# A fused token-mixing and ternary-FFN kernel: a one-power scale for four tiles' statistics, a later wait for the ternary weights, and a prologue with its work dealt out anew

## What is computed

```python
x = L0_attn_x                                   # 8 batches x 1024 tokens x 512 channels, fp32
xn = _layernorm(x)                              # eps 1e-5
x = x + attn(xn) + ffn(xn)

def attn(x):                                    # 16 heads
    xs = jnp.pad(x, ((0, 0), (1, 0), (0, 0)))[:, :T]          # the token before
    xm = x * time_mix + xs * (1.0 - time_mix)
    k = jnp.exp(jnp.minimum(xm @ Wk.T, 60.0)); v = xm @ Wv.T; r = xm @ Wr.T
    # Wm: exponential decay over the lag, one rate a head, own weight at lag 0
    wkv = einsum(Wm, k * v); sum_k = einsum(Wm, k) + 1e-16
    return (sigmoid(r) * wkv / sum_k) @ Wo.T

def ffn(x):
    xn = (x - mean) * rsqrt(var + 1e-3) * ln_gamma + ln_beta
    beta = mean(|weight|); w_q = clip(round(weight / (beta + 1e-5)), -1, 1)   # ternary
    gamma = max(|xn|)                           # over the whole tensor
    return clip(xn * 128 / gamma, -128 + 1e-5, 128 - 1e-5) @ w_q * (gamma * beta / 128)
```

## Time and profile before

| | |
|---|---|
| median of 3 runs | 927.05 us (925.34 to 927.47) |
| the profiled execution's own time | 927.5 us |
| its span in the trace | 925.4 us |
| mean granted TensorE clock | 0.994 |
| PE busy | 879.9 us, 95% of the span |
| DVE busy | 762.3 us, 82% |
| ACT busy | 509.6 us, 55% |
| POOL busy | 207.9 us, 22% |

### The profile page before, as it was taken

How to read it: one execution, slowest core, us unless ns; L and a number is a source line. 1 busy time by engine, 2 the same in 40 slices (tenths; PEclk the granted TensorE clock), 3 DMA queues, 4 the chain that set the end, 5 groups by cost and what they waited for, 6 DMA issues and landing times.

```text
span 925.4 us, 12794 instructions
## 1 busy us (share of the span) xinstructions
PE 879.9 (95%) x3984; PEld 714.7 (77%) x3984; DVE 762.3 (82%) x1278; ACT 509.6 (55%) x832; POOL 207.9 (22%) x268
## 2 busy tenths in 40 slices
PE   2889999999999999999899999999999999999998
PEld 2668777777878777777688888888888888888886
DVE  6898888879798898979689787896878968789684
ACT  5473856747574757747355454554445544456451
POOL 6643425144343425232010020110201102011000
PEclk9999999999999999999899999999999999999999
DMA  7222405142321405144335333353233532244211
GB/s 272 92 91 71 157 14 189 37 148 69 136 91 68 159 0 184 55 147 113 116 124 194 137 94 115 121 193 136 91 104 134 193 136 91 94 145 137 91 46 45
DMA packets 59841, 107.13 MB, mean 116 GB/s; under 512 B 7712, under 2 KB 7712, under 8 KB 59808
## 3 DMA queue, kind: packets, MB, share of 16 engines
q1 hardware_dynamic: 59808, 106.73, 33.9%
HBM read 64.76 MB, written 41.96 MB: 115 GB/s over the span
## 4 chain that ended last, share of the span: by engine, by line
PE 56%; DVE 20%; issue 11%; ACT 7%; POOL 4%; DMA 1%; SPq 0%; DVEq 0%; POOLq 0%; ACTq 0%
PE kvr L483 11%; PE kvr L485 11%; PE kvr L484 11%; PE out_banks L520 6%; PE out_banks L518 6%; DVE scans L921 4%; PE out_banks L498 4%; DVE bn_stats L791 3%; PE out_banks L501 3%; PE out_banks L500 3%; DVE rwkv_lo L941 2%; DVE evacuated L840 2%; DVE k_and_kv L911 1%; DVE k_and_kv L937 1%; DVE absmax L847 1%
## 5 line engine op out<-in xcount | busy, mean ns | idle before, releaser
L1162 POOL TENSOR_TENSOR evacuated<-normed,mix_over_ffn_row 128x512 f32<-128x512 f32 x28 | 36.4, 1298 | 360.5 <-DVE ffn_lo L864 360.5
L483 PE MATMUL kvr<-xm_hi,wk_hi 128*128 128x512 f32 x256 | 104.9, 410 | 8.8 <-ACT w_ternary L753 4.4
L483 PE MATMUL kvr<-xm_hi,wv_hi 128*128 128x512 f32 x256 | 103.4, 404 | 0.1
L483 PE MATMUL kvr<-xm_hi,wr_hi 128*128 128x512 f32 x256 | 102.7, 401 | 0.0
L498 PE MATMUL out_banks<-wo_hi,rwkv_hi 128*128 128x512 f32 x256 | 101.9, 398 | 0.5 <-DVE rwkv_lo L941 0.5
L485 PE MATMUL kvr<-xm_hi,wk_lo 128*128 128x512 f32 x256 | 101.8, 398 | 0.0
L484 PE MATMUL kvr<-xm_lo,wk_hi 128*128 128x512 f32 x256 | 101.4, 396 | 0.0
L501 PE MATMUL out_banks<-wo_hi,rwkv_lo 128*128 128x512 f32 x256 | 101.3, 396 | 0.0
L500 PE MATMUL out_banks<-wo_lo,rwkv_hi 128*128 128x512 f32 x256 | 101.2, 395 | 0.0
L485 PE MATMUL kvr<-xm_hi,wv_lo 128*128 128x512 f32 x256 | 100.3, 392 | 0.0
L484 PE MATMUL kvr<-xm_lo,wv_hi 128*128 128x512 f32 x256 | 100.1, 391 | 0.0
(11 more groups left out here) (119 smaller groups left out, 1915.6 us busy)
## 6 DMA issues: line engine op xcount, KB each, us to landing
other<-ffn_input SPq DMA_DIRECT2D x64, 256.0 KB, 5.3
x<-in_x SPq DMA_DIRECT2D x15, 1024.0 KB, 5.5
other<-in_x SPq DMA_DIRECT2D x8, 1024.0 KB, 5.8
ffn_input<-evacuated SPq DMA_DIRECT2D x32, 256.0 KB, 4.5
ffn_input<-parked SPq DMA_DIRECT2D x32, 256.0 KB, 2.1
attn_scratch<-x SPq DMA_DIRECT2D x8, 1024.0 KB, 4.3
parked<-attn_scratch SPq DMA_DIRECT2D x8, 1024.0 KB, 7.0
out<-parked SPq DMA_DIRECT2D x8, 1024.0 KB, 5.2
```

What stands on the lines that cost most here:

```text
L483: nc.tensor.matmul(KVR[:, m, :], hi, XH[t][:, ch, :], start=(ch == 0), stop=False)
```

## The change

Four edits. The scales of an other tile come from one power of var * (1 + eps2) + eps1 * eps2 (eps1 and eps2 are the two epsilons), so ACT's and POOL's halves of the normalisation come after three steps; the ratio row is computed behind POOL's half, by two more powers. PE's wait for the ternary weights moves from the start of phase B into each `ffn_out`. In the prologue ACT makes only the part with one minus the mix factor, and DVE reads the bank itself, scales and adds; the slots are taken one by one, not in pairs, and PE waits for two mixed slots rather than four evacuated ones. POOL's FFN normalisation of the first tile shrinks from four quarters to two and moves ahead of its casts of Wv and Wo; ACT does the other two. DVE's calls of `mix_or_clip` and `low_part` in the prologue are dealt out as ACT's are, and the power of the row leaves `ffn_scale`; both are left out below.

```diff
@@ PE
             pe.wait_ge(dve_w, CH)
-            pe.wait_ge(act_u, CH)
+            pe.wait_ge(dve_x, 2)
...
                 start_slot = first_slot(f"ffn_{what}", "B")
+                pe.wait_ge(act_q, CH)
                 for ch in range(CH):
...
-            pe.wait_ge(act_q, CH)
             with pe.Fori(HALF, B - 1) as b:
@@ ACT
                 elif mix:
-                    nc.scalar.activation(U[:, r, :], bank, ACT.Copy, scale=tmx[:, ch:ch + 1])
+                    if ph != "P":
+                        nc.scalar.activation(U[:, r, :], bank, ACT.Copy, scale=tmx[:, ch:ch + 1])
...
-                act.wait_ge(pool_step, STEPS + steps_before(i, ph) + (STEPS if ffn else MIX_STEPS))
+                act.wait_ge(pool_step, STEPS + steps_before(i, ph) + (OTHER_STEPS if "other" in kind else STEPS if ffn else MIX_STEPS))
...
-            last.then_inc(act_xn, 2)
+            last.then_inc(act_xn, 1)
             act.wait_ge(dve_c, 2)
-            for pair in range(0, CH, 2):
-                for m in (pair, pair + 1):
-                    evacuate(0, "P", m)
-                for m in (pair, pair + 1):
-                    high_part(0, "P", m)
+            evacuate(0, "P", 0)
+            for m in range(1, CH):
+                evacuate(0, "P", m)
+                high_part(0, "P", m - 1)
+            high_part(0, "P", CH - 1)
+            act.wait_ge(pool_step, STEPS + STEPS)
+            for q in ACT_CHUNKS:
+                last = nc.scalar.activation(XN[:, q, :], X[0][:, q, :], ACT.Identity,
+                                            bias=own[:, 0, 3, q:q + 1], scale=own[:, 0, 2, q:q + 1])
+            last.then_inc(act_xn, 1)
             weight_hi("r")
@@ DVE
-                if kind.startswith("mix") and ph == "B":
+                if ph == "P":
+
+                    bank, scale = first_banks[n], tmx[:, ch:ch + 1]
+                    V.tensor_copy(last_x[:, ch:ch + 1], WS[:, n % 2, TILE - 1:TILE])
+                    V.tensor_scalar(U[:, r, 0:1], bank[:, 0:1], scale, None, ALU.mult)
+                    V.scalar_tensor_tensor(U[:, r, 1:TILE], bank[:, 1:TILE], scale, WS[:, n % 2, 0:TILE - 1],
+                                           ALU.mult, ALU.add).then_inc(dve_x, 1)
+                elif kind.startswith("mix") and ph == "B":
@@ POOL
             ffn_scale(0, 0, own[:, 0])
+            pool.wait_ge(pe_t, CH)
+            normalise(XN, X[0], own[:, 0], 1, pool_xn)
             pool.wait_ge(s_w[1], 16)
             for ch in range(CH):
                 G.tensor_copy(WH["v"][:, ch, :], RAW["v"][:, ch, :]).then_inc(hi_w["v"], 1)
-            pool.wait_ge(pe_t, CH)
-            normalise(XN, X[0], own[:, 0], 1, pool_xn, range(Q))
...
-                mix_scale(*mix_call(b, "A", tile), oth)
-                ffn_scale(*call(b, tile), oth, (b, int(tile[-1])))
+
+
+                i, r = call(b, tile)
+                t = int(tile[-1])
+                mean, var = mv[:, r, :, 0], mv[:, r, :, 1]
+                pool.wait_ge(dve_mv, i + 1)
+                pool.sem_inc(pool_past, 1)
+                G.tensor_scalar(st[:, 5, :], mean, -1.0, 0.0, ALU.mult, ALU.add)
+                step(i, "A", 1, G.tensor_scalar(st[:, 0, :], var, 1.0 + FFN_LN_EPS, LN_EPS * FFN_LN_EPS, ALU.mult,
+                                                ALU.add))
+                step(i, "A", 2, G.tensor_tensor(oth[:, 2, :], st[:, 0, :], half_neg[:, :], ALU.pow))
+                step(i, "A", OTHER_STEPS, G.tensor_tensor(oth[:, 3, :], st[:, 5, :], oth[:, 2, :], ALU.mult))
                 normalise(ZA, ZA, oth, 1, pool_za)
+                step(i, "A", 4, G.tensor_scalar(st[:, 1, :], var, 1.0, LN_EPS, ALU.mult, ALU.add))
+                step(i, "A", 5, G.tensor_tensor(st[:, 2, :], st[:, 1, :], half_neg[:, :], ALU.pow))
+                step(i, "A", 6, G.tensor_tensor(st[:, 3, :], st[:, 0, :], half_pos[:, :], ALU.pow))
+                pool.wait_ge(s_inv[t], 16 * b + 16)
+                G.tensor_tensor(inv[:, t, :], st[:, 3, :], st[:, 2, :], ALU.mult).then_inc(pool_inv, 1)
+                pool.sem_inc(pool_step, STEPS - 6)
```

More of the change, by code:

```diff
@@ L210, in mixed_decay_kernel @@
         pool_max = sem("pool_gamma")
-        STEPS, MIX_STEPS = 9, 3
+        STEPS, MIX_STEPS, OTHER_STEPS = 9, 3, 3
         CREDIT = 1
@@ L875, in _ @@
             weight_lo("k")
-            for pair in range(0, CH, 2):
-                for m in (pair, pair + 1):
-                    mix_or_clip(0, "P", m)
-                for m in (pair, pair + 1):
-                    low_part(0, "P", m)
+            mix_or_clip(0, "P", 0)
+            for m in range(1, CH):
+                mix_or_clip(0, "P", m)
+                low_part(0, "P", m - 1)
+            low_part(0, "P", CH - 1)
             weight_lo("v")
@@ L1084, in mix_scale, with ffn_scale @@
                 step(i, ph, 3, G.tensor_tensor(dst[:, 1, :], st[:, 5, :], dst[:, 0, :], ALU.mult))
-            def ffn_scale(i, r, dst, row=None):
+            def ffn_scale(i, r, dst):
                 var = mv[:, r, :, 1]
@@ L1092, in ffn_scale @@
                 step(i, "A", 6, G.tensor_scalar(st[:, 3, :], st[:, 2, :], 1.0, FFN_LN_EPS, ALU.mult, ALU.add))
-                if row is not None:
-                    b, t = row
-                    pool.wait_ge(s_inv[t], 16 * b + 16)
-                    G.tensor_tensor(inv[:, t, :], st[:, 3, :], half_pos[:, :], ALU.pow).then_inc(pool_inv, 1)
                 step(i, "A", 7, G.tensor_tensor(st[:, 4, :], st[:, 3, :], half_neg[:, :], ALU.pow))
```

## The result

The changed kernel takes 919.79 us (median of 4 runs, 919.36 to 921.01), the kernel before in the same session 927.26 us (925.34 to 927.52, 4 runs). The ratio is 0.9924, 95% interval 0.9908 to 0.9939. It is faster, but by 7.5 us where 15.6 were forecast, and 919.79 lies above the range of 907.5 to 917.5.

A forecast was written before the change was run, and what follows sets the result against it. PE, busy 95% of the span, was taken as the bound, with only its 45.5 idle us to win. 6.4 + 5.2 + 4.0 = 15.6 us off 927.5 gave 911.9, stated as 911.5 for the median, range 907.5 to 917.5.

The forecast's parts named there:

- The late wait: Start of phase B: first `ffn_out` 7.0 us earlier, less a new 0.6 us wait, gives 6.4 us; ends 3.5 and 7.0.
- a new wait of 0.6 us there: Group 9, first batch of phase B: PE arrives at 479.8, the exponential it needs is done about 480.6.
- The first rival: Change of phase: the late chunk of own0 takes over, the late wait yields 2.0 us, time 915.9; chance 0.10.
- the rival in which nothing changes: Whole kernel: stalls come back elsewhere, yield 1.8 + 0 + 0 us, time 925 to 927; chance 0.04.
- The one-power scale: Phase A, other1: ScalarE's wait for POOL goes, 1.3 us a batch, 5.2 us in four; ends 3.6 and 7.4.
- The rival of VectorE as the next bound: Phase A: the wait at 214.01 takes all 1.84 us, batches yield nothing, time 916.7; chance 0.10.
- POOL's tail: Behind each other tile's normalisation: four new POOL instructions hold VectorE's scans, 928 to 931 us, slower; chance 0.04.
- The prologue: First tile: PE's 3.06 us stall and ScalarE's 2.35 us wait go, VectorE 4.0 us earlier; ends 2.5 and 5.4.
- The low part of Wv: Prologue, VectorE: needs the cast of Wv from 22.6 on, cast ends at 24.0, low part ends near 24.7.
- POOL's two quarters: Prologue, POOL's FFN normalisation: two quarters, at 2.1 us each, begin at 16.2 and end near 20.4.

The follow-up runs named there:

- the early load: Kernel before, with SyncE asking for two chunks of own0 right behind the store that ends phase A, nothing else changed: 927.66 us, ratio 1.000.
- four places: Changed kernel with four buffers for the prologue's shifted part, two of them the gate's: 918.95 us, ratio 0.9906.
- in company: Kernel before with one-power scale, late ternary wait and two own0 chunks asked for early: 912.97 us with the prologue part, 915.02 us without.

## Why the prediction was wrong

**The late wait: 6.4 forecast, 0 measured (-1.4 to 1.3 us).** The first half of the step held. The first `ffn_out` began 8.9 us behind the store that ends phase A (454.55 - 445.61) where it had been 16.2 (468.72 - 452.49), at full clock: 7.3 us, forecast 7.0. The step that failed is: "SyncE asks for it behind a chain of stores and loads that hangs on VectorE's adds, not on PE, so it will not land earlier. VectorE then works off the chain that led to the clip", and with it "I take a new wait of 0.6 us there". Its premise is true: the chunk did not land earlier against the store. What fell is the price of the wait behind it. I let the chain run to the clip's old place, 478.06 - 452.49 = 25.6 us behind the store, and had the exponential done at 28.1. In the changed kernel the clip began 472.88 - 445.61 = 27.3 us behind the store, 1.7 later, as much as the chunk landed later, and the exponential was done at 475.95, which is 30.3. The other part of these 2.2 us is a reading: the row at 478.06 is one clip of 1.15 us (x1) and not two, so the first clip is done at 479.2 and not 478.6. The prediction also had nothing for what comes behind: PE waits of 0.25 and 1.26 us, and a granted clock of 0.67 over 4 us and 0.90 over the next 4. An estimate from these rows is 4.1 us of waits and 1.7 us of slow clock, 5.8 of the 7.3 us; from the store to the end the changed kernel kept 0.6 us and the late wait alone 1.0. The rest is not accounted for.

The first rival was the right mechanism with the wrong price (2.0 us left, chance 0.10). Its words "they share the DMA engines with the one that is waited for" fit what is seen, though no run tests them by themselves: SyncE's four issues of own0 took 3.26 us instead of 8.82, and the first chunk 12.75 us to land instead of 10.9. So the chunk landed 19.2 us behind the store where it had been 17.5. "The waited chunk is ahead in the queue" was no argument, as it was not ahead of the 3 MB of x, `normed` and `parked`. The experiments settle that the chunk holds the gain: the late wait yields 0, the early load 0, both 6 to 7. One sum among the rivals does not come out: in the rival in which nothing changes, 458.03 - 456.2 = 1.8 us is how late group 3 would be, and 7.0 - 1.8 = 5.2 us would be left, not 1.8.

**The one-power scale: 5.2 forecast, 5.5 measured.** Right, and the mechanism as well. In the changed kernel a batch gained 1.56 us and not 1.3, since the wait four slots later did not grow by 0.54 us; four such batches would be 6.2 us, so the close agreement of the totals is in part luck. A small wait of 0.21 us appeared a slot ahead. The rival of VectorE as the next bound did not come true, nor did POOL's tail hold VectorE in phase A: POOL's power took up to 2.04 us, and the batch was shorter all the same. In the prologue, with four places, both engines paid: 2.48 and 2.29 us became 4.14 and 4.12. The Trainium skill (SBUF — State Buffer, section SBUF: two separate sides) says that against a GpSimd operation that reads SBUF the lock is taken by VectorE operations with two SBUF inputs too. The rows agree: the subtraction with two inputs is stretched and `bn_stats` with one is not. One input is no safe sign, though. VectorE's clip has one, and in phase B of the traces of before and after all 28 clips that run beside POOL's multiplication of two tiles take 1.13 to 1.24 us, where the 98 others take 0.53 to 0.55. POOL had begun first each time and keeps its 1.29 to 1.31 us (rows at 472.45 and 472.88).

**The prologue: 4.0 forecast, 2.0 in company, 0 alone (-0.4, -1.4 to 0.6).** PE's stall of 3.06 us went, as said. The failed step is "VectorE's part of this stage is dense work in either kernel, so its start on the statistics of the other tile moves from 28.67 to about 27.4". It is not dense: slot by slot with two places for the shifted part, ScalarE and VectorE wait on each other (0.82 and 0.81 us on VectorE). With four places these waits went, and the low parts ended 1.5 us earlier, counted from VectorE's first mixing step. Two further terms were mis-sized. The low part of Wv was put at 22.6 to 24.7, bound by the end of the cast alone, and it takes 3.31 to 4.14 us beside POOL's casts. This is a loss against the forecast and not against the kernel before, where POOL's normalisation ran beside VectorE instead: Wv's and Wr's low parts took 28.67 - 22.61 = 6.1 us there and 29.79 - 24.15 = 5.6 in the changed kernel. And POOL's two quarters took 2.02 us, not 4.2. Why it was worth nothing alone is seen in its trace: all that PE won, ScalarE's wait for POOL took (5.70 us). With the one-power scale beside it that wait is 0.53 us, and 2.0 us come through.

Behind the 2.66 us wait at slot 8 the clock fell in the changed kernel (0.68 in 55 to 59) and not in the kernel before, nor with four parts (1.00 in the same stretch), though the wait was as long. That is about 1 us of the missing ones in this execution, with 15 matmul rows in 4 us where the four-part kernel has 22. It is not the change that does it: of the 17 profiles, 8 keep 1.00 over the 4 us behind the wait at this slot and 9 fall to 0.50 to 0.64, kernels with the old prologue and with the new one among both. What decides it was not settled.

Of the 15.6 us, then: 6.4 lost to the chunk, 2.0 in the prologue, and the one-power scale 0.3 better; 15.6 - 6.4 - 2.0 + 0.3 = 7.5, as measured. Each of these terms is uncertain by 1 us or more, so that the sum comes out to the tenth is luck.

## What to carry to other kernels

When a wait is taken out, follow every transfer and engine chain that does not move with it, and ask for each how much earlier its reader now comes; the first one with less slack than the gain caps it. Here a request for two chunks made earlier was worth 6 to 7 us, and nothing before the wait was gone. A hand-off between two engines with two buffers needs work in between: alternate by pairs, or give it as many buffers as slots. Before a term is read off a prologue, look at how much its start moves from one execution to the next, and count from a start that the compared kernels share.

## What the runs showed of the hardware

A two-input subtraction on VectorE and a cast on POOL stretch each other (2.48 to 4.14 us for four, and 2.29 to 4.12), while `bn_stats` beside the same cast leaves both as they are (2.46 and 2.29). A transfer of 256 KB asked for behind 3 MB of loads took 12.75 us, with 349 GB/s over the stretch. VectorE's clip of 128x512, with one input, took 1.13 to 1.24 us when POOL's two-input operation had begun just before it (28 times in two traces) and 0.53 to 0.55 otherwise (98 times); POOL's operation kept its 1.29 to 1.31 us. PE waits of 1.82 to 2.70 us at the same slot left the granted clock at 1.00 over the next 4 us in 8 profiles and were followed by 0.50 to 0.64 in 9. The start of the first transposes lay between 11.48 and 14.23 us in the 17 profiles, at 11.48 and 12.75 in two of one and the same kernel.
